# Graph network in four layers: a fourth buffer slot for batches of gathered table rows, with the table read back from DRAM

## The reference, cut to what matters

```python
def _gat(x, src, dst, W, a_src, a_dst, b):
    xw = (x @ W).reshape(n, H, FH)                       # H = 4 heads of 32 features
    al_s = jnp.einsum('nhf,hf->nh', xw, a_src)
    al_d = jnp.einsum('nhf,hf->nh', xw, a_dst)
    e = jax.nn.leaky_relu(al_s[src] + al_d[dst], NEG_SLOPE)
    m = jax.ops.segment_max(e, dst, num_segments=n)
    ee = jnp.exp(e - m[dst])
    den = jax.ops.segment_sum(ee, dst, num_segments=n)
    alpha = ee / den[dst]
    out = jax.ops.segment_sum(alpha[:, :, None] * xw[src], dst, num_segments=n)
    return out.reshape(n, H * FH) + b
# src, dst: the 200000 edges and one loop per node; the edges are sorted by dst
h = jax.nn.elu(_bn(_gat(x, src, dst, W1, a1_src, a1_dst, b1), g1, beta1))
h = jax.nn.elu(_bn(_gat(h, src, dst, W2, a2_src, a2_dst, b2), g2, beta2))
```

## Time and profile before

| | |
|---|---|
| median of 3 runs | 9239.11 us (9206.37 to 9263.33) |
| the profiled execution | 9304.56 us, of which its span is 9302.7 us |
| first layers, up to the first gather of the attention loop | 0 to 4076.6 us |
| loop over edges, layer 0 | 4076.6 to about 6366 us |
| end of layer 0, projection of layer 1 | about 6366 to 6714 us |
| loop over edges, layer 1 | 6714 to about 9021 us |
| busy: PE / DVE / ACT / POOL | 52% / 40% / 16% / 41% of the span |

### The profile page before, as it was taken

One profiled execution on the slowest core, in us unless ns is written; L12 is line 12 of the kernel. 1 busy time (PEld: TensorE's weight loads), 2 busy tenths in 40 slices (PEclk: granted clock), 3 DMA queues, 4 the chain that ended last, 5 costly groups with the idle time before them and its releaser, 6 DMA issues.

```text
span 9302.7 us, 89358 instructions
## 1 busy us (share of the span) xinstructions
PE 4882.9 (52%) x36486; PEld 3987.3 (43%) x36587; DVE 3702.3 (40%) x3861; ACT 1513.7 (16%) x2834; POOL 3838.9 (41%) x3489
## 2 busy tenths in 40 slices
PE   7999697996999997713222222223222322223222
PEld 6998485784885554412222222222122222222221
DVE  8999303984002222223333233333333333323245
ACT  3554001000003331101111111110011111111110
POOL 1221000000000000067777777774377777777761
PEclk9999898998999996656655566655555665556565
DMA  4323352453544430024433343342133333334341
GB/s 149 134 122 129 154 199 113 185 200 115 204 179 146 144 120 0 0 45 107 104 95 99 93 106 98 99 101 60 27 87 101 98 99 97 98 88 110 90 100 26
DMA packets 648353, 1005.48 MB, mean 108 GB/s; under 512 B 68889, under 2 KB 523457, under 8 KB 632186
## 3 DMA queue, kind: packets, MB, share of 16 engines
q1 hardware_dynamic: 536138, 761.80, 24.3%
q0 software_dynamic: 111952, 240.24, 10.8%
HBM read 661.45 MB, written 341.93 MB: 108 GB/s over the span
## 4 chain that ended last, share of the span: by engine, by line
PE 30%; issue 19%; POOL 15%; DVE 12%; another core or an unknown queue 10%; ACT 1%; DMA 1%; DVEq 0%; ACTq 0%; SPq 0%; POOLq 0%
POOL arena L636 15%; PE PS L885 13%; PE PS L981 5%; PE PS L875 3%; DVE arena L1562 2%; PE PS L963 2%; PE PS L1083 2%; DVE arena L1571 1%; PE PS L1026 1%; DVE arena L1428 1%; PE PS L1103 1%; PE PS L1111 1%; PE PS L1031 1%; DVE arena L1554 1%
## 5 line engine op out<-in xcount | busy, mean ns | idle before, releaser
L636 POOL DMA_INDIRECT arena<-table,arena x3136 | 3398.3, 1084 | 1144.9 <-issue 951.4
L1083 PE MATMUL PS<-arena 128*128 128x132 f32 x6272 | 1035.0, 340 | 1183.7 <-issue 769.3
L1083 PEld LDWEIGHTS PS<-arena 128*128 128x128 f32 x6272 | 992.9, 249 | 1218.2 <-issue 1058.3
L1549 DVE TENSOR_TENSOR arena<-arena,PS 32x512 f32<-32x512 f32 x98 | 66.2, 675 | 2909.2 <-issue 1585.4
L885 PE MATMUL PS<-arena 128*128 128x256 bf16 (+1 forms) x11025 | 1188.4, 270 | 0.0
L885 PEld LDWEIGHTS PS<-arena 128*128 128x128 bf16 x11025 | 1058.4, 98 | 119.1
L620 POOL DMA_INDIRECT segment_terms<-arena,bias_idx x98 | 95.3, 972 | 1933.7 <-DVE arena L1652 1905.0
L779 ACT ACTIVATE arena<-PS 128x396 f32<-128x396 f32 (+1 forms) x1078 | 525.2, 491 | 2010.6 <-remote 987.6
L1065 PE MATMUL PS<-ident,arena 128*32 128x128 f32 x392 | 93.2, 385 | 1439.8 <-DMA arena<-table,arena 1439.8
L825 PE MATMUL PS<-arena 128*128 128x49 bf16 x7936 | 804.9, 278 | 23.5 <-DVE arena L1276 20.5
L825 PEld LDWEIGHTS PS<-arena 128*128 128x128 bf16 x7936 | 776.7, 150 | 54.7 <-issue 45.2
(11 more groups left out here) (342 smaller groups left out, 5080.6 us busy)
## 6 DMA issues: line engine op xcount, KB each, us to landing
arena<-counts SPq DMA_DIRECT2D x93, 3136.0 KB, 10.3
segment_sums<-arena SPq DMA_DIRECT2D x98, 2176.0 KB
counts<-arena SPq DMA_DIRECT2D x31, 3136.0 KB, 9.4
arena<-counts SPq DMA_DIRECT2D x36, 2048.0 KB, 7.9
arena<-table,arena POOLq DMA_INDIRECT x3136
arena<-counts SPq DMA_DIRECT2D x12, 1792.0 KB, 7.2
table<-arena SPq DMA_DIRECT2D x2, 3332.0 KB
arena<-segment_terms SPq DMA_DIRECT2D x98, 64.0 KB
```

What stands on the lines that cost most here:

```text
L636: g_.indirect_dma_start(out=ring[n % RING][:, i, :], out_offset=None, in_=table_d[j][:, :], in_offset=bass.IndirectOffsetOnAxis(ap=other[: ...
L1083: last = t_.matmul(sums_bank(n, g), onehot[:, g, :], ring[n % RING][:, g, 0:SW], start=True, stop=True)
```

## The change

`RING` is 4. The fourth slot has no room of its own: its place is (6664 + 3 x 4352) modulo 19720 = 0, so it lies over the first 4352 of the 6664 floats of `TAB`, which are 32 of its 49 blocks. So POOL waits, before the first batch of a layer that goes into that slot, until the target scores have been scattered out of `TAB`. At the end of a layer SP reads the whole table back from DRAM into `TAB`, and `combine` waits for that.

```diff
-    RING = 3
+    RING = 4
...
-        ring = [AR(6664 + 4352 * t, 4352).rearrange("p (g r) -> p g r", r=RW) for t in range(RING)]
+        ring = [AR((6664 + 4352 * t) % 19720, 4352).rearrange("p (g r) -> p g r", r=RW) for t in range(RING)]
...
@@ block.sync, the end of layer j @@
                 sp.dma_start(group_reset, group_d).then_inc(s["group_in"], 16)
+                sp.dma_start(TAB, table_d[j].rearrange("(b p) f -> p b f", p=P)).then_inc(s["table_back"], 16)
...
@@ block.gpsimd, the loop over batches @@
                     if k >= RING:
                         pool.wait_ge(s["seg_sums"], GPB * (n - RING + 1))
+                    elif n % RING == RING - 1:
+                        pool.wait_ge(s["bias_set"], 16 * NB * (j + 1))
...
@@ block.vector, combine(j) @@
                 dve.wait_ge(s["own_in"], 16 * NB * (j + 1))
+                dve.wait_ge(s["table_back"], 16 * (j + 1))
```

More of the change, by code:

```diff
@@ L269, in gnn_kernel @@
                      "table_ready", "table_stored", "bias_set", "first_rows", "first_stored", "rows_in_0", "rows_in_1",
-                     "rows_in_2", "terms_in0", "terms_in1", "scores_turned", "scores_taken", "logits", "weights",
+                     "rows_in_2", "rows_in_3", "table_back", "terms_in0", "terms_in1", "scores_turned", "scores_taken", "logits", "weights",
                      "weights_turned", "weights_in", "tops_in", "weighed", "hot_ready", "seg_sums", "sums_taken",
```

## The result

The changed kernel takes 9280.98 us (median of 20 runs, 9230.32 to 9312.69) against 9223.3 us of the kernel before in 20 runs beside it: a ratio of 1.0058, 95% interval 1.0045 to 1.0070. It is 0.6% slower, where 0.3% faster was forecast. What bounds the loops is what bounded them before; what went the wrong way is the price of a spell of late PE reports.

What follows compares the result with a forecast made beforehand. POOL's issuing of gathers was taken to pace both edge loops. From a median of 9239 us, the fourth slot saved 35 us (28 shorter pauses, 7 pushed along) and the read-back added 3, giving 9207 us; range 9100 to 9275.

Steps and rivals of the forecast that it cites:

- What bounds the kernel: Both edge loops: POOL's issuing of gathers sets the pace whatever the slots; waits for a slot cost at most 193.2 us.
- What ends a spell: Edge loops: late PE reports persist until POOL stops; 12 of 14 ended 9 to 10 us after; chance 0.54.
- The first rival: Edge loops: spells end of themselves and the fourth slot bridges them, saving all 193.2 us; 9049 us, chance 0.18.
- 44 us more: Edge loops: spells of late reports last some 44 us longer, as POOL can issue one more batch (44.4 us).
- So a pause shrinks by 2.6 x 0.76 = 2.0 us: POOL's pauses: 2.6 groups need not be done after the stop, at 0.76 us each; 14 pauses save 28 us.
- 2.6 more: Before POOL's stop: PE gets 44.4 / 16.8 = 2.6 groups further during the extra batch.
- the release costs what it did: Lower bound of the fourth slot's saving: nothing, the release behind POOL's stop being unchanged; the upper bound was 193.2 us.
- The 7 us that I had counted for pauses pushed along: Edge loops: 14 spells push pauses along by 3.3 batches, which is half a pause, saving 7 us.
- The read-back: Layer's end: 15 us transfer, done before `combine`, slows first `far` gathers; 3 us in all, bounds 0 and 30.
- The wait for `bias_set`: POOL, ahead of a layer's fourth batch: costs nothing, the scatters being issued at least 136 us earlier.
- More spells: Edge loops, rival: the full four-slot ring brings on more spells, up to 24; 9250 to 9332 us, chance 0.06.
- That they would be there only under a profile: Rival: PE reports late only while profiled, so unprofiled runs have no pauses to save; 9242 us, chance 0.12.

Runs made afterwards that it cites:

- the early wait: POOL waits at a batch's 21st gather for the matmuls of the batch ahead; on the kernel before (three slots) 0.9875, on the changed one (four slots) 0.9905.
- narrow_rows: The kernel before with each gathered row 16 floats instead of 136, plus a memset of the features in the slots; 9351 us, ratio 1.0011.
- before_again: The kernel before, unchanged, run once more for a second profile; 9229 us, ratio 1.0001.
- early_stop3_third: A repeat of the kernel before (three slots) with POOL's wait at the 21st gather, on an occasion without spells; between 1.0000 and 1.0007 of before.
- occasions 2 and 4: Two of six measuring occasions, each with the unchanged kernel before run beside the others; before took 9218 us on 2 and 9021 us on 4.

## Why the prediction was wrong

**What bounds the kernel: right.** The gathers take 3382 us of POOL (3398 before) and the 0.30 us gaps 953.8 (951.4). Only the waits move. On the occasions without spells there are no waits, and the fourth slot brings nothing.

**What ends a spell: right.** Spells end behind POOL's stop with two, three and four slots, and when the stop was moved the end moved with it (the early wait). Only one, ahead of batch 82 of the changed kernel, ended a few us after POOL had resumed from 12.1 us of pause. The first rival, full bridging by a fourth slot (9049 us), has fallen. Spells do last longer: from their first signs to POOL's stop about 62 to 106 us in before's profiles and about 95 to 150 us with four slots, where I had said 44 us more; and the first pause of a layer stands ahead of batch 4.

**"So a pause shrinks by 2.6 x 0.76 = 2.0 us": this step failed.** I took the release behind POOL's stop, 9 to 10 us, as fixed. It is not, and it goes by how many gathers POOL is ahead of PE when it stops: 2.2 to 2.9 us with 20 (the early wait), 4.0 to 5.1 us with 32 (two slots), 8.9 to 9.9 us with 64 (three slots, rows of 64 bytes included), 14.3 to 15.9 us with 96 (four slots). Where a spell has two pauses, the first pause and the second's release are added; alone that second release is 4.0 to 13.3 us. That is some 0.14 us for each gather, an estimate from these four. How long a spell lasted does not matter: with three slots, spells of 62 to 106 us are all released after 8.9 to 9.8 us in before's profiles. Spells that start in the projection take longer, 12 to 16 us with three slots and 17 to 20 with four. So the fourth slot made each release some 5 us longer, where the sum had 2.0 us less. The part that I did count was not far off: ahead of the first pause of layer 0, PE had 6 groups of the awaited batch out when POOL stopped, against 4 before, where I had said 2.6 more. My bound "the release costs what it did" was thus on the wrong side; "zero saving" was no lower bound. The 12 and 16 us at batches 3 and 52 had been a hint that the release is not one number. Why PE takes the longer to be released the more gathers are out stays open.

**What the sum left out.** A spell that begins shortly before the last gather of a layer costs no pause but a tail: 54.8 us in layer 0 above, against 25 to 29 us with three slots in `narrow_rows`, one filled batch of 20.4 us more and the longer release. And a spell that crosses from one batch into the next takes two pauses, such as 10.0 and 12.6 us ahead of batches 13 and 14. Over all, a spell cost 193.2 / 14 = 13.8 and 124.1 / 11 = 11.3 us with three slots, and (112.1 + 54.8) / 7 = 23.8 and 121.1 / 6 = 20.2 us with four. That the only tail in these profiles fell to four slots is chance; without it the 23.8 is 112.1 / 6 = 18.7 us.

**How many spells: open.** The four-slot profiles have 7 and 6 spells, those of before 14 and 11 (the kernel with the read-back only had 10). They can't be held against the timed medians, though: the profiled executions of the changed kernel were faster than its median both times. An estimate from spans: without its pauses and tail the changed kernel comes to 9261.8 - 166.9 = 9095 and 9215.0 - 121.1 = 9094 us, before to 9302.7 - 193.2 = 9110 and 9234.1 - 124.1 = 9110. The medians of 9281 and 9262 then hold 8.5 and 7.6 spells of 22 us, those of 9223 and 9218 hold 9.0 and 8.6 of 12.5 us. So at nearly as many spells each costs some 10 us more, less the 15 us by which the changed kernel is shorter apart from its spells: about +60 us, of the size measured. (Of the 15 us, 10 to 16 are a shorter busy time of the gathers; why is not shown, and without spells it is 3385 us with three slots and with four.) This is no proof: the 22 and the 12.5 us come from two profiles each, the 22 with the tail in it, and the count of spells in typical runs is inferred from them, not seen. The 7 us that I had counted for pauses pushed along can be neither confirmed nor refuted by so few spells. The pieces were seen: the longer release, the double pause, the tail.

**The read-back: right.** It landed in 16.2 us (15 forecast); PE waited 36.50 us for the `far` rows against 36.23, and `combine` began without waiting for it. The wait for `bias_set` cost nothing. (In layer 1 it stands ahead of the third batch and not the fourth, batch 51 being the first in slot 3, so its lead was 13 + 64 gathers, 96 us, and not 136.) With the slot's place these are the parts that three occasions without spells put at nothing together.

**The rivals.** "More spells" had the right sign, and its 9250 to 9332 us hold the measured time, but by the wrong mechanism: the profiles show 7 and 6 spells and not 17 or more, and each became dearer. That they would be there only under a profile can't be told with certainty, since each timed run comes with a recorded clock. But what they cost in a profile is about what the times lose between occasions. Beside `before_again` (span 9234.1 us) I put `early_stop3_third`, the three slots whose early wait never had to wait (9023.4 us): their first stages are equally long, and the pauses (124 us), the longer projection (POOL is away for 376.8 us between the loops, against 335.4), the longer end (309.4 against 274.3) and 10 us more in the loops make the difference of 211 us. The medians of before on occasions 2 and 4 differ by 9218 - 9021 = 197 us.

## What to carry to other kernels

A deeper ring helps only against a wait that ends by itself. Where the consumer is released only once the producer has stopped, as here, every further slot lets the producer run further ahead, and the price comes back as a longer release or as a tail. Fewer slots were no cure either: two cost as much as three, in more and shorter pauses. A wait that stops the producer as soon as the consumer is late was worth 1.2% on the one occasion with spells on which it ran, and nothing where there were none. And before a few per cent are explained, the kernel before should be measured on several occasions: here they differ by 3.5%, six times the effect of the change.

## What the hardware showed that I had not expected

- While POOL issues indirect DMAs one behind the other and PE runs many small instructions, PE's reports can come late until one group of 12 instructions (6 loads, 6 products) takes 16.8 us, 1.40 us for each instruction, though its products as recorded take 1.69 us. With a third of the products no such spell starts in the loops; with rows of 64 bytes they start as before.
- It lasts until POOL stops, and PE is released 2.2 to 2.9, 4.0 to 5.1, 8.9 to 9.9 or 14.3 to 15.9 us of standing still later, with 20, 32, 64 or 96 gathers issued ahead of the batch that PE is on, however long the spell was. Behind a spell from the projection it takes longer, up to 20 us.
- It is there on some occasions (before at 9218 to 9337 us) and absent from every profile of others (9021 us, runs within 10 us of their median), with the same program. What differs between occasions no run here shows.
- Stops of mostly 2.5 to 2.7 us, many of them every other batch, were enough to keep the lag from ever reaching its full rhythm in the profile of either early wait.
